# Second attention layer: four of six causal masks of the second pass added by VectorE in PSUM, one product for skip and centre, two-input sums on GpSimd

## The reference, cut to what matters

```
qk = xn @ qk_w + qk_b;  v = xn @ v_w          # 16 heads of 8 channels
scores = q k^T / sqrt(8), causal mask (row >= column), softmax -> attn
uniform[t, s] = 1/(t+1) for s <= t
new_attn = resid_gain*attn + skip_gain*eye - centre_gain*uniform   # gains per head
s = (new_attn @ v) @ cproj_w
g = silu(xn @ W^T + b + (xn @ V_r) @ C^T)
x = x + s * g
```

## Time and profile before

| what | value |
|---|---|
| runs | 998.69 us median of 3 (994.81 to 999.81) |
| the profiled execution | 1001.72 us |
| its span, first to last instruction | 999.9 us |
| TensorE busy | 786.2 us, 79% |
| VectorE busy | 645.5 us, 65% |
| ScalarE busy | 509.3 us, 51% |
| GpSimd busy | 411.4 us, 41% |
| mean granted TensorE clock | 0.929 |

### The profile page before, as it was taken

One profiled execution on the slowest core, in us unless ns is written; L12 is line 12 of the kernel. 1 busy time (PEld: TensorE's weight loads), 2 busy tenths in 40 slices (PEclk: granted clock), 3 DMA queues, 4 the chain that ended last, 5 costly groups with the idle time before them and its releaser, 6 DMA issues.

```text
span 999.9 us, 19881 instructions
## 1 busy us (share of the span) xinstructions
PE 786.2 (79%) x6259; PEld 506.5 (51%) x6278; DVE 645.5 (65%) x1137; ACT 509.3 (51%) x883; POOL 411.4 (41%) x394
## 2 busy tenths in 40 slices
PE   0894787989988998854999999525598898989984
PEld 0652444555554554422555555314476666666663
DVE  6552786887788778832655655366356767676763
ACT  1243254676677766642433433258365555555542
POOL 7006776554555454421777777673210101010000
PEclk9996899999999999986999999856799999999997
DMA  5595745444544453142212222240665646464621
GB/s 141 194 192 138 174 121 123 97 94 102 123 115 92 100 122 88 31 136 59 58 53 53 58 55 54 78 122 16 142 135 124 148 117 159 115 157 117 136 58 51
DMA packets 132671, 106.13 MB, mean 106 GB/s; under 512 B 23317, under 2 KB 124633, under 8 KB 129545
## 3 DMA queue, kind: packets, MB, share of 16 engines
q1 hardware_dynamic: 122348, 91.23, 39.8%
q0 software_dynamic: 4352, 8.99, 2.9%
q10 hardware_dynamic: 5920, 5.24, 1.7%
HBM read 54.60 MB, written 50.03 MB: 105 GB/s over the span
## 4 chain that ended last, share of the span: by engine, by line
PE 27%; DMA 10%; DVE 7%; issue 4%; ACT 4%; SPq 2%; POOL 1%; DVEq 0%; ACTq 0%; POOLq 0%
PE ps L671 8%; DMA od_d<-ev 5%; PE ps L692 3%; PE ps L1567 3%; DVE mx L1272 3%; DMA rec<-od_d 2%; PE ps L683 2%; PE ps L665 2%; PE ps L1576 1%; ACT rows L893 1%; PE ps L673 1%; PE ps L1519 1%; SPq L1113 1%; PE ps L1517 1%; PE ps L1545 1%
## 5 line engine op out<-in xcount | busy, mean ns | idle before, releaser
L1272 DVE TENSOR_REDUCE mx<-ps 128x4 f32<-128x1024 f32 (+1 forms) x224 | 268.4, 1212 | 146.8 <-PE ps L1513 69.9
L1423 ACT ACTIVATE probs<-probs 128x1024 f32<-128x1024 f32 x128 | 131.8, 1051 | 64.9 <-DVE probs L1282 63.6
L1428 ACT ACTIVATE probs<-ps 128x1024 f32<-128x1024 f32 x96 | 96.8, 1024 | 82.9 <-PE ps L1545 55.8
L1202 POOL TENSOR_TENSOR qkr<-qkf,qk 128x512 f32<-128x512 f32 x27 | 31.3, 1160 | 244.0 <-ACT qk L1392 238.4
L1230 POOL TENSOR_TENSOR probs<-probs,tabB 128x1024 f32<-128x1024 f32 x42 | 99.5, 2369 | 74.6 <-ACT probs L1435 74.6
L1511 PE MATMUL ps<-tabA,eyeb 128*128 128x512 bf16 x256 | 102.3, 399 | 25.9 <-DMA ks<-parts_d 10.9
L1567 PE MATMUL ps<-probs,vpad 128*32 128x256 f32 (+1 forms) x2048 | 118.7, 362 | 4.2 <-ACT probs L1423 3.6
L1282 DVE TENSOR_TENSOR probs<-ps,tabB 128x1024 f32<-128x1024 f32 x86 | 101.5, 1210 | 4.3 <-PE ps L1539 4.3
L1513 PE MATMUL ps<-ks,qs 96*128 96x256 bf16 x512 | 102.3, 282 | 0.0
L1539 PE MATMUL ps<-qs,ks 99*128 99x256 bf16 x512 | 77.2, 280 | 6.8 <-DMA qs<-mT 2.6
L671 PE MATMUL ps<-qs,probs 128*128 x144 | 80.9, 644 | 1.4
(11 more groups left out here) (226 smaller groups left out, 1530.1 us busy)
## 6 DMA issues: line engine op xcount, KB each, us to landing
parts_d<-qk SPq DMA_DIRECT2D x64, 192.0 KB, 4.3
qs<-parts_d SPq DMA_DIRECT2D x32, 384.0 KB, 5.0
ks<-parts_d SPq DMA_DIRECT2D x32, 384.0 KB, 6.7
parts_d<-qk SPq DMA_DIRECT2D x64, 128.0 KB, 3.2
od_d<-ev SPq DMA_DIRECT2D x64, 128.0 KB
slots_in<-probs SPq DMA_DIRECT2D x1, 4680.0 KB
probs<-slots_in SPq DMA_DIRECT2D x72, 65.0 KB, 1.8
parts_d<-qk SPq DMA_DIRECT2D x64, 64.0 KB, 1.9
```

The lines of the kernel that those rows point to most:

```text
L1272: nc.vector.tensor_reduce(mx[:, s.buf(), t, heads[0]:heads[-1] + 1], ring[:, slot].rearrange("p (h n) -> p h n", n=w), AX.X, ALU.max).then ...
L1423: nc.scalar.activation(probs[:, j, :], probs[:, j, :], ACT.Exp).then_inc(exp_done, 1)
L1428: nc.scalar.activation(probs[:, j, :], ring[:, slot], ACT.Exp).then_inc(exp_done, 1)
```

## The change

For layer 1 only (layer 0 keeps its order):

- Units B0 to B3 get no mask product. Each matmul starts its own sum, and VectorE adds the mask table to the 128 diagonal columns of each of the four heads, in PSUM (`causal`); ScalarE's exponential of these units waits for that (`masked`). Units 4 and 5 and the first pass keep their mask products.
- `wvs` becomes v's weights times resid, and is used for V; so the scaling needs no resid. E is one product, with plain v weights. VectorE takes its running sum and adds skip (a column of `cols`) times it; minus centre is multiplied into `v.share` once, by GpSimd, ahead of the layer.
- GpSimd takes over the copy of the batch's tokens (`tokens`), the scaling (`scale`), the product with 1/(t+1) and the last sum (`running_mean`), the split of the maxima (`parts_gpsimd`) and the residual (`residual`).
- Positions: late values 2, 3 ahead of position 2 and 4, 5 ahead of position 4 (before: all four ahead of 0); values 0 and 1 after position 8 (before 9); QK ahead of 3 (before 1); V ahead of 5 (before 4); the turn ahead of 11 (before after 11); `invert` after 11 (before 7). ScalarE: query-key parts at 3 (1), evacuation of the output at 4 (0), the copies of v at 5, behind the exponential of B1 (4), the copy of the turned maxima at 10 (after 11). VectorE: `add_shape` ahead of A4's maximum (behind it). SP: parts 1 and 2 together, maxima ahead of the inverses.

```diff
@@ setup
-            nc.vector.tensor_copy(v.cols[:, 4:6], ps[:, 2, 4:6]).then_inc(small_cp, 1)
+            nc.vector.tensor_copy(v.cols[:, 4:7], ps[:, 2, 4:7]).then_inc(small_cp, 1)
...
+            nc.vector.tensor_tensor(v.wvs[:].rearrange("p (h d) -> p h d", d=HD),
+                                    v.wv1[:].rearrange("p (h d) -> p h d", d=HD),
+                                    gains[:, 0, :].unsqueeze(2).broadcast_to([P, H, HD]), ALU.mult).then_inc(copied, 1)
@@ middle, gpsimd
+        nc.gpsimd.tensor_scalar(v.share, v.share, v.cols[:, 6:7], None, ALU.mult).then_inc(cleared, 1)
@@ attention
-    LATE = 2 if layer else 4
-    SCALE = 2 if layer else 0
-    INVERT = 7 if layer else 10
-    VALUES = {9: (0, 1)} if layer else {13: (0, 1), 15: (2, 3)}
+    LATE = {2: (2, 3), 4: (4, 5)} if layer else {1: (4, 5), 3: (6, 7)}
+    VALUES = {8: (0, 1)} if layer else {13: (0, 1), 15: (2, 3)}
+    SCALE, INVERT, PROJECT = (None, 11, 10) if layer else (0, 10, 8)
+    QK, V, TURN = (3, 5, 11) if layer else (1, 4, NU * 2)
...
+    A_PART, A_OUT, A_TWO, A_VAL, A_MAX = (3, 4, 4, 5, 10) if layer else (2, 4, 4, 4, NU * 2)
@@ sync
+                else:
+                    if s.has(2):
+                        parts(s, 0)
+                    if s.has(-2):
+                        outputs_out(s)
+                    if s.has(2):
+                        parts(s, 1)
+                        parts(s, 2)
+                    if s.has(-2):
+                        sums_in(s)
+                        outputs_in(s)
+                    if s.has():
+                        maxima(s)
+                    if s.has(-2):
+                        inverses_out(s)
+                        inverses_in(s)
@@ gpsimd
+            def tokens(s):
+
+                if s.has(-1):
+                    pool.wait_ge(v_full, s.n(-1) + 1)
+                nc.gpsimd.tensor_copy(xb[:], xnT[:, bass.ds(s.n() * T, T)]).then_inc(xb_done, 1)
+
+            def scale(s):
...
+                nc.gpsimd.tensor_tensor(on[:], raw[:], rden[:], ALU.mult).then_inc(on_done, 1)
+
+            def running_mean(s):
+
+                pool.wait_ge(e_evac, 2 * (s.n(-3) + 1))
+                nc.gpsimd.tensor_tensor(cum[:], cum[:], v.share, ALU.mult).then_inc(shaped, 1)
+                pool.wait_ge(shaped, 2 * s.n(-3) + 1)
+                nc.gpsimd.tensor_tensor(on[:], on[:], cum[:], ALU.add).then_inc(shaped, 1)
+
+            def residual(s):
+
+                y = yt[:].rearrange("p (c d) -> p c d", c=2)
+                pool.wait_ge(y_evac, s.n(-3) + 1)
+                nc.gpsimd.tensor_tensor(y, x[:, bass.ds(s.n(-3) * 2, 2), :], y, ALU.add).then_inc(fin_done, 1)
+
+            def second_body(s):
+                if s.has():
+                    tokens(s)
+                if s.has(2):
+                    rest_one(pool, nc.gpsimd, s)
+                if s.has(-3):
+                    scale(s)
+                if s.has(2):
+                    rest_two(pool, nc.gpsimd, s)
+                if s.has(-3):
+                    running_mean(s)
+                if s.has():
+                    parts_gpsimd(pool, s)
+                if s.has(-3):
+                    residual(s)
@@ vector
             def add_shape(s):
 
                 dve.wait_ge(e_full, s.n(-3) + 1)
+                if s.has(-4):
+                    dve.wait_ge(shaped, 2 * (s.n(-4) + 1))
+                nc.vector.tensor_tensor_scan(cum[:], v.onesT[:], misc[:, 0:T], 0.0, ALU.mult, ALU.add).then_inc(e_evac, 1)
                 dve.wait_ge(on_done, s.n(-3) + 1)
...
+                nc.vector.scalar_tensor_tensor(on[:], misc[:, 0:T], cols[:, 5:6], on[:], ALU.mult, ALU.add
+                                               ).then_inc(e_evac, 1)
+
+            def causal(s, j, slot):
+
+                dve.wait_ge(full["B"], NU * s.n(-1) + j + 1)
+                diagonal = ring[:, slot].rearrange("p (h n) -> p h n", n=T)[:, :, 0:P]
+                nc.vector.tensor_tensor(diagonal, diagonal, maskB[:].unsqueeze(1).broadcast_to([P, 4, P]), ALU.add
+                                        ).then_inc(masked, 1)
@@ scalar
                 else:
-                    act.wait_ge(full["B"], NU * s.n(-1) + j + 1)
+                    if j < 4:
+                        act.wait_ge(masked, 4 * s.n(-1) + j + 1)
+                    else:
+                        act.wait_ge(full["B"], NU * s.n(-1) + j + 1)
...
-                    if pos == 4 and s.has():
+                    if pos == A_VAL and s.has():
                         values(s)
+                    if pos == A_MAX and s.has():
+                        max_rows(s)
@@ tensor
-                    elif w == T:
-                        if n % 2 == 0:
-                            diagonal = o[:, T * n:T * n + 2 * T].rearrange("p (h t) -> p h t", t=T)[:, :, 0:P]
-                            nc.tensor.matmul(diagonal, eyeb[:], maskB[:].unsqueeze(1).broadcast_to([P, 2, P]),
-                                             start=True, stop=False, skip_group_check=True)
-                        mm = nc.tensor.matmul(at, k, qs[0:MROW + PARTS, b, h, :], start=False, stop=True, skip_group_check=True)
...
-                        nc.tensor.matmul(misc[:, 0:T], v.wvs[:], batch_tokens(s, -3), start=True, stop=True)
-                        nc.tensor.matmul(misc[:, T:2 * T], v.wv1[:, 1, :], batch_tokens(s, -3), start=True, stop=True
-                                         ).then_inc(e_full, 1)
+                        nc.tensor.matmul(misc[:, 0:T], v.wv1[:], batch_tokens(s, -3), start=True, stop=True).then_inc(e_full, 1)
```

More of the change, by code:

```diff
@@ L1165, in body @@
                     stacks(s)
[L1166 to L1181, removed]
+                if layer == 0:
+                    if s.has(2):
[16 more added lines that the diff above has]
+                    if s.has(2):
+                        parts(s, 0)
+                    if s.has(-2):
+                        outputs_out(s)
+                    if s.has(2):
+                        parts(s, 1)
+                        parts(s, 2)
+                    if s.has(-2):
+                        sums_in(s)
+                        outputs_in(s)
+                    if s.has():
+                        maxima(s)
+                    if s.has(-2):
+                        inverses_out(s)
+                        inverses_in(s)
             if layer:
@@ L1351, in body @@
                         scale(s)
+                    if layer and pos == 6 and s.has(-3):
+                        add_shape(s)
                     if U.exists(s.k, kind):
@@ L1356, in body @@
                             add_bias(s, j, U.slot(s.k, pos))
-                    if kind == "A" and j == NU - 1 and s.has() and (layer or s.k < HELP):
+                        elif layer and j < 4:
+                            causal(s, j, U.slot(s.k, pos))
+                    if kind == "A" and j == NU - 1 and s.has() and (layer == 0 and s.k < HELP):
                         maximum_parts(s)
-                    if layer and pos == 6 and s.has(-3):
-                        add_shape(s)
                     if pos == INVERT and s.has(-2):
@@ L1448, in body @@
             def body(s):
-                if s.has():
+                if layer == 0 and s.has():
                     if s.has(-1):
@@ L1474, in body @@
                     act.dma_start(v.wdn, v.down_w.rearrange("e (c i) h -> i e c h", c=2)).then_inc(v.w_load, 16)
-                if s.has():
+                if A_MAX >= len(U.order) and s.has():
                     max_rows(s)
@@ L1615, in body @@
                         mm.then_inc(y_full, 1)
+                    if pos == TURN and s.has():
+                        turn_maxima(s)
                     if U.exists(s.k, kind):
@@ L1620, in body @@
                             values(s, -1, i)
-                if s.has():
-                    misc_free(pe, s, "M")
-                    pe.wait_ge(max_parts, 4 * (s.n() + 1))
-                    nc.tensor.transpose(misc[0:PARTS * 2 * H, 0:P // 2].bitcast(BF16),
-                                        m3[:].rearrange("p c h t -> p (c h t)"), eyeb[:]).then_inc(mt_full, 1)
+                if TURN >= len(U.order) and s.has():
+                    turn_maxima(s)
             if layer:
```

113 lines of the change are left out of this document (52 added, 61 removed).

## The result

The changed kernel takes 1032.61 us (median of 4 runs, 1031.26 to 1033.86), beside 999.0 for the kernel before on the same chip: ratio 1.0345, 95% interval 1.0312 to 1.0378. I had forecast 999.0, with 1013 as the upper end. It is slower, and outside the range. One of the four executions of the last experiment, e10_best, took 1274.5 us at a mean granted clock of 0.57; it is kept out of that experiment's ratio (the median of the other three is 978.72), and no reading rests on it.

What follows compares the result with a forecast made beforehand. TensorE was taken as nearest the bound, at 16.65 us a step; 3.2 us removed nearly met 3.05 of new waits plus 0.1. Eleven steps at -0.5 and edges at +0.5 gave 0.0: 999.0 us, range 986 to 1013.

Steps and rivals of the forecast that it cites:

- E's new wait of 2.6 us: Each step: TensorE stands 2.6 us before E until ScalarE, behind B1's exponential, has copied V.
- the rival that I gave 0.05: Waits at E lower TensorE's granted clock in each step, making the kernel slower: 1026 us, chance 0.05.
- the wait at 750: TensorE's 2.5 us wait at 750 us in the old trace, clock 1.00; cited against a clock loss.
- 2.1 us lost in 13 steps: Clock loss if each wait at E dropped it as in the layer's first stretch, giving 1026 us; chance 0.05.
- +1.7: Drain: later B0 and waits for B1's and B5's exponentials, less 0.4 of products, add 1.7 us together.
- +0.75: Last output: scaling, sums and residual on GpSimd and hand-offs, less an earlier scan, add 0.75 us.
- The schedule behind it: Full loop step laid out from A0 to its end, waits at E and turn included: 16.6 us, was 16.65.
- The 0.4 that three steps were to hold for the loop's jump: Three of eleven loop steps hold some 0.4 us each for the jump, now between B5 and A0.
- 826.60 to 826.72: Start-to-start distance pricing one mask product on TensorE at 0.11 us; eight removed per step save 0.88.
- -2.5: Step 2: its 2.53 us gap before B5 goes as the reciprocal moves; the step is 13.8, from 16.27.
- B0 waits for the maxima's DMA: Sign against the forecast: B0 held by a maxima transfer over 3.5 us; at 4.5, 1.0 a step, 1012 us.
- a step is 13.5 plus 0.4: Rival: evacuations reach E in time, TensorE stays the bound, -2.8 us a step over eleven, 968 us; chance 0.09.

Runs made afterwards that it cites:

- e10_best: Changed kernel with V's copies ahead of B1's exponential, late values earlier after the last input, E later, last two steps' scaling, sums, residual on VectorE: 979.23 us, ratio 0.9795.
- e1_fill10: Changed kernel with ten throwaway identity products on TensorE ahead of E's unchanged wait: 1009.46 us, ratio 1.013.
- e5: Changed kernel with V's copies ahead of B1's exponential and the residual back on VectorE: 991.86 us, ratio 0.9903.
- e4: Changed kernel with V one position earlier on TensorE and its copies first in ScalarE's work of position 4: 991.14 us, ratio 0.9909.
- e2: Changed kernel with ScalarE's two copies of V moved back ahead of B1's exponential: 988.86 us, ratio 0.9916.
- e9: Changed kernel with V's copies ahead of B1's exponential and the four masks as TensorE products again: 987.36 us, ratio 0.9882.
- e7_wait4: Kernel before, with TensorE made to wait at E's place for four small GpSimd sums each step: 1029.75 us, ratio 1.0295.
- e7_wait7: Kernel before, with TensorE made to wait at E's place for seven small GpSimd sums each step: 1053.87 us, ratio 1.0539.
- e1_fill4: Changed kernel with four throwaway identity products on TensorE ahead of E's unchanged wait: 1011.45 us, ratio 1.0146.
- e3: Changed kernel with the four masks as TensorE products again: 1002.37 us, ratio 1.0038.
- e8: Changed kernel with V's copies ahead of B1's exponential and, after the last input, all four late values ahead of position 2: 991.22 us, ratio 0.9914.
- e6: Kernel before, with only the four mask additions moved to VectorE: 1070.46 us, ratio 1.0713.

## Why the prediction was wrong

**The step that failed** is the clock, which the sum puts at nothing: E's new wait of 2.6 us was laid into every step with the granted clock at 1.00 behind it. The reason stands under the rival that I gave 0.05: "Against: the wait at 750 was as long and dropped nothing." The length was right, the conclusion was not. The same trace holds the wait of 2.89 at 724.02 with the clock at its lower level behind it, and I did not weigh it. In the changed kernel step 3's wait (2.43) dropped nothing, and each one from step 4 on did (2.60, and 2.43 in the last three). One wait that drops nothing does not show that others of its length drop nothing.

The term of that rival was "2.1 us lost in 13 steps", 27 us; measured are none in step 3, then 2.4 and 1.25 us in turn (19.35 and 18.18 for 16.93), 24 us in all. So its price was near and its chance was wrong. That the price was near is in part luck: it came from one stretch of 4.2 us at the layer's start, and the stretches here are 6.7 and 3.9. The section HAM oscillation of the Trainium skill's page "TensorE: Matmul & The Clock Gate", which I set aside, warned in the right direction: a wait repeated in a loop can lower the clock each time, and here it does at 2.6 us, in every step from 4 on.

**The second failed term is the drain**, "+1.7" and "+0.75" for 7.7 at full clock. (The parts named for the first, 0.35, 1.1 and 1 less 0.4, make 2.05.) Measured in e1_fill10 against before: 3.9 us is the distance from the last operation to the end of the span, which no term held. That it goes with GpSimd's last operation is shown by e5 and e10; what the engine or the profile does in these 6.2 us is not. The last evacuation on ScalarE comes 14.45 behind the last turn for 13.18 (+1.3, forecast +1.7); its transfer is issued 1.7 us behind the evacuation for 0.7 (+1.0); the reciprocal, the scaling and the path behind Y add 0.8, 0.3 and 0.3. Each of these is a difference of rows; what delays the transfer was not settled.

**What was right, and what was a little off:**
- The wait: "one gap of some 2.6 us a step ahead of E, its releaser ScalarE's evacuation of V" is 2.60 and 2.61, from L1471.
- The schedule behind it: step 3 is 16.73, the steps of e1_fill10 are 16.93, for 16.62. Of the 0.3 over, some 0.25 lies between the turn and E (10.82 for 10.57), the rest behind E (6.11 for 6.05). There GpSimd's four parts release the turn after a wait of 0.24 (forecast 0.45). The 0.4 that three steps were to hold for the loop's jump shows in none: steps 4 to 12 of e1_fill10 are 16.91 to 16.95.
- The mask product "826.60 to 826.72" is 0.12 us and not 0.11; other rows give either, and nothing hangs on it.
- The additions, 0.694 for 0.67; the sum of one product (L1370) 0.46 for 0.44; VectorE's share of a step falls from 11.9 to 11.2 us (130.50 and 122.93 over eleven steps), forecast 0.5 less.
- Step 2: 14.06 for 13.8, so that "-2.5" was -2.2.
- GpSimd: scaling, sums and residual 0.72 to 0.73 for 0.74; the token copy (L1273) was 0.40 for 0.74, without effect. The maxima did not grow beside it: 1.218 us in the mean (e1_fill10, L1336) for 1.212 before (L1272).
- The maxima: their transfer holds B0 up in no step of the loop. "B0 waits for the maxima's DMA" did not come.
- The case in which E did not wait, "a step is 13.5 plus 0.4", was too low, and with it the 968. In e4, where E hardly waits, a step is 14.9 to 15.3, with a wait of up to 0.79 for B1's exponential in its place, which a sum of TensorE's work alone could not show.

## What to carry to other kernels

Before calling a wait harmless because its sum is unchanged, ask what the waiting engine's clock does with it: merging the gaps of 1.47 and 0.4 us of a step into one of 2.6 kept the schedule and cost 24 us. Look at every long wait of the trace and at the clock behind it, not at one; and where a wait is under suspicion, fill it with throwaway products, which separates the clock from the wait in one run. Where a new operation reuses a buffer, look whose place in another engine's queue releases it; here a copy behind one exponential decided over 44 us. Moving work from a near-full engine to one inside the chain need not help: with or without the additions on VectorE the mended kernel takes the same time (e2 and e9).

## What the runs showed of the hardware

- TensorE's granted clock fell to 1.2 GHz behind waits of 2.89 (before, end of step 0), 2.60 in steps 4 to 12 and 2.43 in steps 13 to 15 (after), 2.12 once (e5), 1.3 to 1.5 with one of 1.1 to 1.3 shortly ahead, in eight of eleven steps, and 1.39 once without it (e7_wait4). It stayed at 1.00 behind 2.53 (before, step 2), 2.43 (after, step 3), 2.33 twice (e7_wait7), some 1.7 (e1_fill4), 1.5 (e3) and 0.9 (e2) in every step. Neither the length of one wait nor its repetition sorts these. What does, and why the lower clock then lasts 6.7 us in one step and 3.9 in the next, is not settled.
- The span of every kernel whose GpSimd worked in the last 8 us ended 6.2 us behind GpSimd's last operation (6.25, 6.24, 6.21, 6.2, 6.2, 6.18, 6.19, 6.17, 6.22 in after, e1_fill10, e1_fill4, e2, e3, e4, e5, e8 and e9). Where it had stopped long before, the end was 2.3 to 2.4 us behind VectorE's last operation (before, both e7, e6, e10).
